# Graph aggregation from plain counts in two products, with the degree scale moved into the features

## What is computed

```python
xn = layernorm(x)
# graph convolution: what the change touches
row, col = concat(src, arange(n)), concat(dst, arange(n))   # every node has a loop
deg  = segment_sum(ones, col);  dinv = rsqrt(deg)
h    = xn @ W
g    = segment_sum(h[row] * (dinv[row] * dinv[col]), col) + b
# attention of 12 heads with weights 1 + A + A*A/2, and its projection
x1   = x + g + attention(xn) @ w_proj + b_proj
# a switch layer of 8 experts (capacity 195) over layernorm(x1), added to x1
```

## Time and profile before

| | us |
|---|---|
| runs (3) | 1078.35, 1080.57, 1081.0; median 1080.57 |
| the profiled execution, its own time | 1076.3 |
| its span in the trace | 1074.5 |
| TensorE busy | 928.6 (86%) |
| VectorE busy | 778.9 (72%) |
| ScalarE busy | 482.1 (45%) |
| POOL busy | 352.3 (33%) |
| mean granted TensorE clock | 0.952 of full |

### The profile page before, as it was taken

One profiled execution on the slowest core, in us unless ns is written; L12 is line 12 of the kernel. 1 busy time (PEld: TensorE's weight loads), 2 busy tenths in 40 slices (PEclk: granted clock), 3 DMA queues, 4 the chain that ended last, 5 costly groups with the idle time before them and its releaser, 6 DMA issues.

```text
span 1074.5 us, 15640 instructions
## 1 busy us (share of the span) xinstructions
PE 928.6 (86%) x5294; PEld 884.8 (82%) x5294; DVE 778.9 (72%) x1553; ACT 482.1 (45%) x710; POOL 352.3 (33%) x233
## 2 busy tenths in 40 slices
PE   2896799999999999999998679789999996498985
PEld 2896788888888888888887579789999996398885
DVE  6869169888889889889888825665666767467673
ACT  2311266666666766766767402111323223165640
POOL 2025556544545545545345000000000001435562
PEclk9998899999999999999999989989999996589998
DMA  9966452472462462472353194465556533568761
GB/s 278 338 163 152 78 109 19 73 145 29 72 141 33 72 137 36 72 144 29 72 87 91 47 175 119 105 155 145 143 155 159 153 116 130 145 194 265 244 219 46
DMA packets 137406, 136.65 MB, mean 127 GB/s; under 512 B 70361, under 2 KB 118076, under 8 KB 136337
## 3 DMA queue, kind: packets, MB, share of 16 engines
q1 hardware_dynamic: 109550, 119.23, 42.1%
q0 software_dynamic: 27408, 16.66, 10.1%
q10 hardware_dynamic: 403, 0.17, 0.1%
HBM read 94.27 MB, written 38.14 MB: 123 GB/s over the span
## 4 chain that ended last, share of the span: by engine, by line
PE 55%; DVE 19%; issue 11%; ACT 6%; DMA 5%; POOL 1%; SPq 1%; DVEq 0%; ACTq 0%; POOLq 0%
PE ps L1873 13%; PE ps L1874 12%; PE ps L1875 12%; PE ps L1146 6%; DVE Pl L1005 3%; PE ps L1130 3%; PE ps L1131 3%; DVE Ph L1003 3%; DMA out<-oE,ids 2%; ACT Ph L793 2%; ACT Pf L815 2%; PE ps L1512 1%; DVE eqp L958 1%; DMA Cs<-counts 1%; PE ps L1106 1%
## 5 line engine op out<-in xcount | busy, mean ns | idle before, releaser
L365 POOL DMA_INDIRECT counts<-countc,idxu x157 | 269.0, 1713 | 289.8 <-DMA counts<-countc,idxu 197.6
L1005 DVE SCALAR_TENSOR_TENSOR Pl<-Pf,Ph 125x832 fp32r<-125x832 f32 (+1 forms) x180 | 184.0, 1027 | 51.3 <-ACT Ph L793 47.4
L815 ACT ACTIVATE Pf<-ps 125x832 f32<-125x832 f32 (+1 forms) x180 | 156.0, 867 | 129.7 <-PE ps L1131 120.0
L1146 PE MATMUL ps<-Ph,vsb 125*128 125x416 f32 (+1 forms) x360 | 131.2, 365 | 22.6 <-DVE Pl L1005 22.5
L1146 PE MATMUL ps<-Pl,vsb 125*128 125x416 f32 (+1 forms) x360 | 126.7, 352 | 0.0
L1146 PEld LDWEIGHTS ps<-Ph,vsb 125*128 125x128 f32 x360 | 67.7, 188 | 36.0 <-DVE Pl L1005 21.2
L1873 PE MATMUL ps<-wH,XH 128*125 128x384 f32 x240 | 84.3, 351 | 9.9 <-DVE OHL L950 5.8
L1873 PE MATMUL ps<-XH,wqkH 128*128 128x416 f32 (+1 forms) x216 | 83.0, 384 | 9.8 <-DVE wqkL L862 8.1
L1874 PE MATMUL ps<-wL,XH 128*125 128x384 f32 x240 | 83.0, 346 | 0.0
L1875 PE MATMUL ps<-wH,XL 128*125 128x384 f32 x240 | 82.8, 345 | 0.0
L793 ACT ACTIVATE Ph<-Pf 125x832 fp32r<-125x832 f32 (+1 forms) x90 | 80.5, 896 | 0.7
(11 more groups left out here) (254 smaller groups left out, 2276.3 us busy)
## 6 DMA issues: line engine op xcount, KB each, us to landing
Cs<-counts SPq DMA_DIRECT2D x20, 546.9 KB
w1s<-L_ffn_w SPq DMA_DIRECT2D x8, 1152.0 KB, 6.1
w2s<-L_ffn_w SPq DMA_DIRECT2D x8, 1152.0 KB, 5.7
odram<-OHL SPq DMA_DIRECT2D x12, 625.0 KB, 7.7
oS<-odram SPq DMA_DIRECT2D x10, 750.0 KB, 4.8
vdram<-VS SPq DMA_DIRECT2D x10, 672.0 KB
vsb<-vdram SPq DMA_DIRECT2D x12, 560.0 KB
kt<-keyd SPq DMA_DIRECT2D x5, 1280.0 KB, 6.0
```

The lines of the kernel that those rows point to most:

```text
L365: pool.indirect_dma_start(out=counts, out_offset=bass.IndirectOffsetOnAxis(ap=idxu[:, c:c + 1], axis=0), in_=countc[:, c:c + 1], in_offset ...
L815: act.activation(Pf[:, i % RING, :, 0:w], ps[0:T, 2 * (i % 2):2 * (i % 2) + 2, 0:w], ACT.Square, bias=1.0).then_inc(sq_done, 1)
L1005: dve.scalar_tensor_tensor(out=p, in0=f, scalar=1.0, in1=h.bitcast(F32), op0=ALU.add, op1=ALU.subtract).then_inc(p_lo, 1)
L1146: ins = pe.matmul(ps[:, 4 + s % 2, 0:w], vsb[:, 2 * kp + t, a, :], part[:, m % RING, t, 0:w], start=(kp == 0 and t == 0 and part is Ph), s ...
```

## The change

1. The loops' ones are written into `counts` in DRAM: after the zeros, two DMAs on POOL's queue write 1249 separate words and one last word of the diagonal. All scatters wait for them (`CLEARED` goes from 48 to 80; `ZEROED` = 48 is what the other engines wait for).
2. The aggregation's matrix is the plain count, rounded once by ScalarE straight from the loaded block. `Csc` and `CL` are gone, and with them the identity's add. The dinv of the source is applied to the features: ScalarE copies each group from PSUM to `raw` in fp32, and once dinv is known it writes HH = round(dinv * raw) and VectorE HL = dinv * raw - HH. The gather has two matmuls a block: CH x HH and CH x HL.
3. A count of 4096 or more may lose bits in CH. At most four source rows can have one (20000 // 4096). They are found on the chip from the maxima (`peak`, `heavy`), numbered (`heavy_ranks`, `heavy_numbers`: 10 + 10 small fp32 matmuls), fetched by POOL, and their low parts go through `lowd` in DRAM into partitions 125 and 126 of blocks 8 and 9 of CH (`load_low`), beside copies of those rows of HH (`heavy_rows`, 20 matmuls of 384 columns, then `hc`). All this is executed whether or not such rows exist.
4. The column sums are four adds over halves instead of one strided reduce, with a maximum ahead of them.
5. Order: TensorE starts the features without `pairs_over`, and uses other PSUM banks for the degrees; SP issues the first two count loads in the last turn of the pair loop, ahead of odram's last stores; `degrees(i)` follows group i + 2; dinv is formed after group 12; gnn_b's load moves behind the features. The eq_done and padded semaphores are replaced by others with the same meaning.

```diff
+            pool.wait_ge(scattered, ZEROED)
+            pool.dma_start(counts[0:(N - 1) * (N + 1)].rearrange("(s d) o -> s (d o)", d=N + 1)[:, 0:1].rearrange(
+                "(a p) o -> a (p o)", a=1), ones2[0:1, 0:1].broadcast_to([1, N - 1]), allow_slow_non_contiguous=True).then_inc(scattered, 16)
+            pool.dma_start(counts[N * N - 1:N * N, :], ones2[0:1, 0:1]).then_inc(scattered, 16)
...
                     load_w3(sp, 5)
+                    sp.wait_ge(sc_done, PAIRS * STEPS)
+                    sp.wait_ge(p_lo, PAIRS * STEPS)
+                    sp.wait_ge(scattered, CLEARED + 16 * ET)
+                    load_counts(sp, 0)
+                    load_counts(sp, 1)
                 sp.wait_ge(o_fin, 3 * j + 3)
...
+            def load_low(i):
+
+                for s_, q in SPARE:
+                    sp.dma_start(CH[T:T + 2, i % 2, s_, :].bitcast(F32), lowd[q:q + 2, i * T:(i + 1) * T]).then_inc(low_in[i % 2], 16)
...
+            for q in range(2, NT + 1):
+                load_counts(sp, q)
                 if q in (2, 3):
                     load_w3(sp, 4 + q)
+            sp.wait_ge(heavy_ready, 4)
+            sp.dma_start(lowd[:, :], rows).then_inc(low_in[1], 16)
+            sp.dma_start(bgp[:], gnn_b.rearrange("(a d) -> a d", a=1).broadcast_to([T, D])).then_inc(bias_in, 16)
+            sp.wait_ge(low_in[1], 16)
+            load_counts(sp, NT + 1)
             sp.wait_ge(h_mm, 2 * NT)
-            load_counts(NT)
+            load_low(0)
+            load_low(1)
...
                 if i == 0:
                     load_w3(sp, 8)
+                    sp.wait_ge(heavy_ready, 5)
+                    for s_, q in SPARE:
+                        sp.dma_start(HH[T:T + 2, s_, :].bitcast(F32), hc[q:q + 2, :]).then_inc(low_in[0], 16)
...
+            def scale_rows(i):
+                act.wait_ge(h_raw, 2 * i + 2)
+                act.activation(HH[0:T, i, :], raw[:, i, :], ACT.Copy, scale=dinv[:, i:i + 1]).then_inc(h_hi, 1)
...
-                act.activation(CH[:, i % 2], Csc[:], ACT.Copy).then_inc(ch_done, 1)
+                act.activation(CH[0:T, i % 2], Cs[:, q % 2], ACT.Copy).then_inc(ch_done, 1)
...
+            def degrees(i):
+                dve.wait_ge(cs_in[i % 2], MOVED * (i // 2 + 1))
+                if i >= 2:
+                    dve.wait_ge(deg_mm, i - 1)
+                part = Cs[:, i % 2]
+                order(dve.tensor_reduce(peak[:, i, :], part, AX.X, ALU.max))
+                order(dve.tensor_tensor(part[:, 0:5, :], part[:, 0:5, :], part[:, 5:10, :], ALU.add))
+                order(dve.tensor_tensor(part[:, 0:2, :], part[:, 0:2, :], part[:, 2:4, :], ALU.add))
+                order(dve.tensor_tensor(part[:, 0, :], part[:, 0, :], part[:, 1, :], ALU.add))
+                dve.tensor_tensor(csum[:, i % 2, 0:T], part[:, 0, :], part[:, 4, :], ALU.add).then_inc(csum_done, 1)
+
+            def low_rows(i):
+                dve.wait_ge(h_hi, i + 1)
+                dve.scalar_tensor_tensor(out=HL[:, i, :], in0=raw[:, i, :], scalar=dinv[:, i:i + 1],
+                                         in1=HH[0:T, i, :].bitcast(F32), op0=ALU.mult, op1=ALU.subtract).then_inc(h_lo, 1)
...
-            pairs_over(pe)
-            pe.wait_ge(oacc_done, 6 * PAIRS + FREE)
+            pe.wait_ge(sq_done, PAIRS * STEPS)
+            pe.wait_ge(inv_row, PAIRS)
+            pe.wait_ge(kq_full, 6 * PAIRS)
             pe.wait_ge(w_lo, 6)
...
+            def heavy_rows():
+
+                pe.wait_ge(heavy_ready, 4)
+                pe.wait_ge(h_hi, NT)
+                for c in range(2):
+                    for t in range(NT):
+                        ins = pe.matmul(ps[0:HEAVY, 6 + c, 0:HALF], seatr[:, t, :], HH[0:T, t, c * HALF:(c + 1) * HALF],
+                                        start=(t == 0), stop=(t == NT - 1))
+                ins.then_inc(heavy_mm, 1)
+
+            def gather(i, c, tiles):
+
+                b = 2 * (i % 2) + c
+                for s_ in tiles:
+                    k = T + 2 if s_ >= SPARE[0][0] else T
+                    cs = slice(c * HALF, (c + 1) * HALF)
+                    pe.matmul(ps[0:T, b, 0:HALF], CH[0:k, i % 2, s_, :], HH[0:k, s_, cs], start=(s_ == 0), stop=False)
+                    ins = pe.matmul(ps[0:T, b, 0:HALF], CH[0:T, i % 2, s_, :], HL[:, s_, cs], start=False, stop=(s_ == NT - 1))
+                return ins
...
+                if g >= DEGREE_LAG and g - DEGREE_LAG < NT:
+                    degrees(g - DEGREE_LAG)
+                if g == DEGREES_AT:
+                    heavy_ranks()
+                if g == DEGREES_AT + 2:
+                    heavy_numbers()
...
+                if i == 0:
+                    pe.wait_ge(h_lo, SPARE[0][0])
+                    gather(0, 0, range(SPARE[0][0]))
+                    heavy_rows()
+                    gather(0, 1, range(SPARE[0][0]))
+                    pe.wait_ge(h_lo, NT)
+                    pe.wait_ge(low_in[0], 64)
+                    for c in range(2):
+                        ins = gather(0, c, range(SPARE[0][0], NT))
+                else:
+                    pe.wait_ge(low_in[i % 2], (64 if i % 2 == 0 else 16) + 32 * ((i + 1) // 2))
+                    for c in range(2):
+                        ins = gather(i, c, range(NT))
                 ins.then_inc(agg_mm, 1)
```

More of the change, by code:

```diff
@@ L100, in build @@
 def build(nc, x, src, dst, gnn_w, gnn_b, w_qkv, b_qkv, w_proj, b_proj, sw, sb_, w1, b1, w2, b2, out,
-          counts, keyd, vdram, odram, xfd, x1d, invd):
+          counts, keyd, vdram, odram, xfd, x1d, invd, lowd):
     ctx = ExitStack()
@@ L1282, in _ @@
             round_counts(0)
+            for i in range(scaled, NT):
+                scale_rows(i)
+            round_counts(1)
             hi_w3(act, 8)
@@ new lines, in _ @@
+            for i in range(2):
+                low_rows(i)
+            dve.wait_ge(heavy_mm, 2)
+            order(dve.memset(rows, 0.0))
+            dve.tensor_scalar(hid[:, 0:1], ps[0:HEAVY, 6, 16:17], FAR, None, ALU.add).then_inc(heavy_ready, 1)
+            for i in range(2, LOW_AT):
+                low_rows(i)
+            dve.wait_ge(rows_in, 16)
+            for c0 in range(0, N, 4 * T):
+                n = min(4 * T, N - c0)
+                order(dve.tensor_copy(low[:, 0:n], rows[:, c0:c0 + n]))
+                ins = dve.tensor_tensor(rows[:, c0:c0 + n], rows[:, c0:c0 + n], low[:, 0:n].bitcast(F32), ALU.subtract)
+                if c0 + n < N:
+                    order(ins)
@@ L1347, in logits @@
+            ins.then_inc(heavy_ready, 1)
+            for i in range(LOW_AT, NT):
+                low_rows(i)
             def logits(i):
```

197 lines of the change are left out of this document (108 added, 89 removed).

## The result

The changed kernel takes **1048.08 us** (median of 4 runs, 1044.9 to 1054.38) against 1080.78 of the kernel before, measured beside it: a ratio of 0.9692, 95% interval 0.9659 to 0.9725. The forecast was 1041, its range 1031 to 1062, so the sign and the range held, and the time came out 7 us above the point. The profiled execution took 1044.9 (span 1043.2). The forecast for a profiled execution was 1036.3, so 8.6 us have to be found.

What follows compares the result with a forecast made beforehand. TensorE bounds aggregation and projection but waits around the features' stage: 1076.3 profiled - 31.6 (third product) - 9.9 (earlier tile 1) + 1.5 (near ties) = 1036.3; with 4.3 carried to the median, 1040.6, say 1041; range 1031 to 1062.

Steps and rivals of the forecast that it cites:

- Part 1: Aggregation tiles 1 to 9: dropping the third product saves 31.6 us, all on the path, as TensorE has no idle time.
- near ties: Aggregation tiles: VectorE's 15.1 us loop and other loops nearly as long as TensorE's some 16.0; 1.5 us charged for nine tiles.
- Part 2: Features' stage: starts 5.9 us earlier, but degrees pace it; last feature at 688.8 against 690.2, early start eaten up.
- Rival 2: Dear maxima in the features' stage: 4.5 us a count tile, last sum 6 to 8 us later, 1048; chance 0.15.
- The step that failed: Features' stage, later count tiles: a load takes 3.6 us from the sum freeing its buffer; VectorE's 3.4 to 3.5 sets pace.
- The features' start: End of the pair loop: TensorE begins the features at 609.6 instead of 615.47, no longer waiting for the last output's folding.
- Part 3: Turn into the aggregation: tile 1 starts 21.6 us after the last feature, at 710.4, 9.9 us earlier than before.
- its range's lower end: Features' stage: TensorE never held by the sums, last feature 8 us earlier, 1033 in the forecast's own range.
- Part 4: Diagonal's ones written on POOL's queue before the scatters: up to 43 us hidden, 3 us and a landing expected, nothing charged.
- Rivals 3 and 4: Diagonal write: one DMA engine does it all (chance 0.09), or each word pays its latency, 1120 at 100 ns (0.05).
- Rival 1: VectorE and its store become the bound in the aggregation tiles: 17.2 us a tile, 12 more, 1053; chance 0.12.
- rival 3: One DMA engine writes the diagonal: 49 us, 6 over the cover, 10 with issue and landing, 1048 to 1052; chance 0.09.

Runs made afterwards that it cites:

- Counts before store: Changed kernel with the last output's store and two projection weight loads moved behind the third and fourth count loads on SP's queue: 1051.4 us, 0.9738.
- tables early: Changed kernel with the two small routing tables' loads moved on SP's queue to behind the pair loop's last weight load: 1045.6 us, 0.9674.
- all three: Changed kernel with the edits of tables early, Buffer freed early and degrees 5 behind together: 1049.4 us, 0.9708.
- Buffer freed early: Changed kernel with the first add writing to free memory, so a count buffer is given back after the maximum and one add: 1041.6 us, 0.9635.
- degrees 5 behind: Changed kernel with each degree product issued 5 groups behind on TensorE's queue instead of 2, each sum with its own buffer: 1048.0 us, 0.9672.

## Why the prediction was right, and where it was not

**Part 1 was right, in mechanism and size.** Expected 31.6 us less 1.5 for near ties; measured 32.2 in the nine tiles, and 3.53 us a tile when the product was put back. The near ties cost nothing: TensorE is busy for 140.76 of 140.76 us. The argument that VectorE's loop would come down to some 15.1 us carried as much as the product's columns: with the old loop the same two products take 17.7 a tile. The forecast booked all of the gain on the product and treated the loop as a danger, which gives the right sum, but hides that 18.6 of the 32.2 us are lost without the shorter loop.

**Part 2 was right in its unit costs and wrong in its pace.** Maximum 1.46 us (1.4 said), count tile 3.4 (3.4), first two sums without a wait, TensorE's wait for the third 7.1 (5 said), 29.6 us from the reading of the maxima to E (29.3; the small fp32 products took 2.9 of it, not 4.0, and a granted clock of 0.95 there made up for them). The Trainium skill's "VectorE: DVE Perf Modes", "The perf-mode tier table", had a reduction at an element a cycle; 1.46 us for 1250 elements is just what the subtraction of 1250 takes, so this trace agrees. The 2.53 of before is a sum, reads with a stride and writes 125 elements instead of 10; that the stride makes the difference is likely and not shown. Rival 2 is out. The step that failed is "from then on a load takes 3.6 us ... and VectorE's 3.4 to 3.5 is the pace". The 3.6 was read from where a load's traffic ended in a window, not from a wait that the load ended. In the changed kernel the eighth sum is done at 661.46 and its buffer is ready again for the tenth maximum at 666.58, 5.1 us later: the last packet ends 4.2 us after the sum, and 0.9 more pass until VectorE is released. With two buffers that makes (3.4 + 5.1) / 2 = 4.3 us a tile late in the stage, where the forecast had (3.4 + 3.6) / 2 = 3.5. Counted from the features' start, the third sum comes 1.8 us later than forecast, the fifth 2.1 (beside the store and the weights it is 4.9 to 5.7 a tile, which the forecast had allowed for), the tenth 5.4, and E 6.0, the largest of the differences. So 3.4 us of the 6.0 are the failed step. "Counts before store", "tables early" and "all three" show that the early part is DMA time. "Buffer freed early" shows the late part by its size: a buffer is held for 2.3 us instead of 3.4, (2.3 + 5.1) / 2 = 3.7, and 3.6 was measured.

**The features' start** was put at 609.6, the place of one execution. It came at 615.15, in spite of the 5.85 us of waiting that did go, because that execution's pair loop ended 5.5 us later at a lower granted clock. Taking a border of an unchanged stage from one execution was the weakness, not Part 2's first step.

**Part 3 was right to 1.2 us** (22.8 against 21.6), with both its chains seen: weights at E + 15.8 (low part written at 716.19; 15.3 said, though the terms given, 4.5 + 7.23 + 3.3, add up to 15.0), and the last eight gather products, which wait for hc's rows, from E + 14.7 (13 said). That it is so close is in part luck: the same code took up to 27.4 us in other executions. What it did not see is that both hang on the last sum as much as on E; had E come early, as its range's lower end had it, nothing would have been gained (degrees 5 behind).

**Part 4 was right**: the write is hidden. Its packets take 6.0 us of 16 engines' time instead of 3 (95.6 us in all) and it lands after 10. Rivals 3 and 4 are out. Rival 1 is out too: no idle TensorE in the tiles. (For rival 3 the prediction's own terms, 6 to 10 us, give 1047 to 1051, not 1048 to 1052.)

**The median.** The 4.3 us from the profiled execution to the median of before were carried over; for the changed kernel it is 3.2.

Not settled: why the granted clock falls in the pair loop in one execution and not in another. The runs show only that it does so whatever is edited behind it. That the point came within 7 us is partly this luck, and partly two errors of -2 that took off from +5.5, +6.0 and +1.2.

## What to carry to other kernels

When a profile shows an engine waiting, ask what the end of the stage is counted from before removing the wait: moving the degree products took away most of TensorE's waits, and the time stood still, as the chain began at the last column sum. When a product is dropped, look at the second-longest loop first; here the edit paid fully only because it shortened VectorE's loop too. And take a load's latency from a wait that it ended, not from the end of its packets (3.6 against 5.1 us here), and from a stretch as busy as the one that it will move to: beside the store and the weights it was about 10.

## What the hardware did that was not expected

- The same unchanged pair loop ended anywhere between 609.4 and 621.4 us from the span's start over the executions profiled, with stretches at 0.62 to 0.68 granted clock in which TensorE was as busy as ever; the mean granted clock up to there was 0.98 in the earliest and 0.96 in the latest. That is a larger spread than what several of the edits here are worth.
- A pair of count loads cost SP 1.01 us to issue at 713.77 (DMA share 0.12), and 4.67 us at 625.47 (share 1.33; 6.13 in the run with the third product back). The share alone doesn't tell: at 638.79 it was 1.20 and the issue took 0.94. In the slow cases a store and other loads of SP's had been issued in the few us before; what exactly holds the queue is not shown.
- A write of 1249 single words with a stride went out as 16 packets of 64 words and 16 of 15, and landed in 10 us.
- A contiguous maximum over 1250 elements takes 1.46 us; the sum of before, read with a stride, 2.53.
